# A fused cross-attention and MLP block on one core: the first unit's value matmuls moved between its scores, and half of the projection weights' low parts moved later on VectorE

## What is computed

```python
def reference_block(x, context, xa_mask, ...):        # x 2 x 2048 x 512, context 2 x 77 x 512, 16 heads of 32
    xq = layer_norm(x, qn_w, qn_b)
    ctx = layer_norm(context, cn_w, cn_b)
    q = (xq @ q_w)                                    # 512 x 512
    k, v = split(ctx @ kv_w)                          # 512 x 1024
    attn = softmax(where(xa_mask, -max, q . k * scale))   # over the 77 context rows, per head
    x = x + (attn . v) @ proj_w + proj_b
    h = layer_norm(x, n2_w, n2_b)
    return x + gelu(h @ fc1_w + fc1_b) @ fc2_w + fc2_b    # hidden size 2048
```

## Time and profile before

| | |
|---|---|
| device time, median of 3 runs | 1047.71 us (1047.18 to 1049.47) |
| profiled execution, its own time | 1051.2 us |
| its span | 1049.3 us |
| TensorE busy | 1033.1 us (98%) |
| VectorE busy | 822.3 us (78%) |
| ScalarE busy | 434.5 us (41%) |
| GpSimd busy | 359.2 us (34%) |

### The profile page before, as it was taken

One profiled execution on the slowest core, in us unless ns is written; L12 is line 12 of the kernel. 1 busy time (PEld: TensorE's weight loads), 2 busy tenths in 40 slices (PEclk: granted clock), 3 DMA queues, 4 the chain that ended last, 5 costly groups with the idle time before them and its releaser, 6 DMA issues.

```text
span 1049.3 us, 16369 instructions
## 1 busy us (share of the span) xinstructions
PE 1033.1 (98%) x5857; PEld 857.7 (82%) x5857; DVE 822.3 (78%) x1323; ACT 434.5 (41%) x766; POOL 359.2 (34%) x259
## 2 busy tenths in 40 slices
PE   8999999999999999999999999999999999999998
PEld 6788888888888777888778888878888888888887
DVE  7899999999997898887877676676766677666655
ACT  4344344444444566445533343342433352232221
POOL 3466566667787673233404000303100310300000
PEclk9999999999999999999999999999999999999999
DMA  7012122122210277564557535345536343834312
GB/s 267 8 47 71 51 92 74 63 62 83 81 42 22 74 297 233 188 232 160 197 213 258 225 131 191 124 159 174 227 131 234 118 164 126 312 120 172 124 67 81
DMA packets 52800, 149.33 MB, mean 142 GB/s; under 512 B 11313, under 2 KB 19545, under 8 KB 44531
## 3 DMA queue, kind: packets, MB, share of 16 engines
q1 hardware_dynamic: 52139, 147.25, 39.3%
q10 hardware_dynamic: 584, 1.06, 0.3%
HBM read 108.13 MB, written 39.85 MB: 141 GB/s over the span
## 4 chain that ended last, share of the span: by engine, by line
PE 93%; DVE 4%; issue 1%; DMA 0%; ACT 0%; POOL 0%; SPq 0%; DVEq 0%; ACTq 0%
PE bank L1801 32%; PE bank L1771 28%; PE bank L1604 8%; PE bank L1648 8%; PE bank L1585 5%; PE bank L1636 4%; PE bank L1617 3%; PE bank L1780 1%; PE bank L1595 1%; PE bank L1567 1%; PE bank L1625 1%; DVE acc L1409 1%; DVE hop L1371 1%; DVE gT L1401 1%; DVE w1r L1366 1%
## 5 line engine op out<-in xcount | busy, mean ns | idle before, releaser
L1801 PE MATMUL bank<-w2r,gT 128*128 128x512 f32 x1536 | 359.7, 391 | 2.2 <-DVE acc L1409 2.0
L1801 PEld LDWEIGHTS bank<-w2r,gT 128*128 128x128 f32 x1536 | 286.7, 188 | 64.2 <-DVE acc L1409 5.1
L1771 PE MATMUL bank<-hop,w1r 128*128 128x512 f32 x1344 | 314.2, 392 | 4.0 <-DVE hop L1371 3.0
L1771 PEld LDWEIGHTS bank<-hop,w1r 128*128 128x128 f32 x1344 | 252.3, 189 | 58.2 <-issue 4.9
L1409 DVE TENSOR_TENSOR acc<-bank,acc 128x512 f32<-128x512 f32 x256 | 176.7, 691 | 103.8 <-PE bank L1801 97.9
L1396 DVE TENSOR_TENSOR ybuf<-bank,ybuf 128x512 f32<-128x512 f32 x224 | 148.6, 688 | 82.3 <-PE bank L1771 74.2
L1046 ACT ACTIVATE ybuf<-ybuf,cols 128x512 f32<-128x512 f32 x128 | 91.6, 716 | 155.5 <-DVE ybuf L1396 155.5
L684 POOL TENSOR_TENSOR S<-S,rsum 128x1232 f32<-128x1232 f32 x32 | 75.3, 2354 | 61.6 <-DVE rsum L1202 61.6
L1401 DVE TENSOR_TENSOR gT<-ybuf,gT 128x512 fp32r<-128x512 f32 x128 | 92.9, 747 | 0.0
L649 POOL TENSOR_TENSOR hrs<-hve,mhalf 128x1 f32<-128x1 f32 x32 | 18.0, 562 | 213.6 <-DVE hve L1381 213.6
L792 POOL TENSOR_TENSOR acc<-acc,fc2b 128x512 f32<-128x512 f32 x32 | 44.0, 1391 | 134.7 <-DMA acc<-x_scratch 134.6
(11 more groups left out here) (111 smaller groups left out, 1450.8 us busy)
## 6 DMA issues: line engine op xcount, KB each, us to landing
w1r<-w_scratch SPq DMA_DIRECT2D x24, 1792.0 KB, 7.3
w2r<-w_scratch SPq DMA_DIRECT2D x24, 1024.0 KB, 5.4
w_scratch<-w1r SPq DMA_DIRECT2D x8, 1792.0 KB, 6.2
xr<-in_x SPq DMA_DIRECT2D x32, 256.0 KB, 2.9
x_scratch<-xr SPq DMA_DIRECT2D x32, 256.0 KB, 2.0
hring<-x_scratch SPq DMA_DIRECT2D x32, 256.0 KB, 3.0
acc<-x_scratch SPq DMA_DIRECT2D x32, 256.0 KB, 4.0
w_scratch<-w2r SPq DMA_DIRECT2D x8, 1024.0 KB, 4.9
```

The lines of the kernel that those rows point to most:

```text
L1771: mm = pe.matmul(bank_[:, :], w1r[:, w1_slot(s), c, w, kk * P:(kk + 1) * P], hop[i][:, d, kk, :], start=(kk == 0 and n == 0), stop=(kk == ...
L1801: mm = pe.matmul(bY[t % 2][:, :], gT[s % 2][:, j, d, t * P:(t + 1) * P], w2r[:, s % 2, j, w, :], start=(n == 0), stop=(n == 5))
```

## The change

Two edits, both in the preparation. On TensorE `values(0)` moves ahead of `x_T(1)`: it stood after the fourth score of tile 0, and now stands after the second. On VectorE two of the four `wpl` instructions stay where all four were (`prep="q"`, ahead of `q_lo(0)`), and the other two go into `prep="scores"`, between `q_lo(0)` and `exp_sum(1)`.

```diff
@@ vector_program, step, prep == "q"
                 keys_lo(1)
                 q_bias()
-                proj_weights(range(KT))
+                proj_weights((0, 1))
                 q_lo(0)
@@ vector_program, step, prep == "scores"
                 recip(0)
                 q_lo(0)
+                proj_weights((2, 3))
                 exp_sum(1)
@@ tensor_program, step, prep == "scores"
                 score(0, 0)
                 score(0, 1)
+                values(0)
                 x_T(1)
                 score(0, 2)
                 score(0, 3)
-                values(0)
                 for g_ in range(KT):
```

## The result

The changed kernel takes 1051.87 us (median of 7 runs, 1051.36 to 1052.66), the one before 1047.18 us (7 runs, 1046.09 to 1049.47). The ratio is 1.0047, with a 95% interval of 1.0036 to 1.0058: 4.7 us slower. In a second comparison the same changed kernel gave 1.0051 (1.0035 to 1.0066). The forecast was 1053.4 us.

A forecast was written before the change was run, and what follows sets the result against it. TensorE was taken to bound the loop, with VectorE nearly the bound in the preparation. Terms 0.0 (waits ahead of q) + 3.8 (wpl beside probs(0)) + 1.9 (clock) = +5.7 us on 1047.7 gave 1053.4 us, range 1049.4 to 1055.3.

The forecast's parts named there:

- TensorE has no slack in the loop: Loop: TensorE, busy for all 60.00 us from 60 to 120 us, can't hide a late start at its first score.
- Edit 1 and 2 sum to zero at q: Preparation, TensorE ahead of q: two waits of 1.5 us come back as one of 1.8 us, sum 0.0 us.
- The two wpl beside probs(0): VectorE ahead of exp_sum(1): wpl and GpSimd's probs(0) take turns, 3.46 us; exp_sum(1) and first score +3.8 us.
- edit 2: values(0) earlier on TensorE: masked(0, 2) and what follows it on VectorE and GpSimd come 1.67 us later.
- the bounds 0.7 and 6: Limits on the +3.8 us at exp_sum(1): 0.7 with normed() clear of GpSimd, 6 with a further GpSimd turn.
- The clock: Start of the loop: TensorE idle 3.9 us, then its granted clock falls, +1.9 us; bounds 0 and twice that.
- the row at 702 us: Earlier trace, loop: 2.29 us wait before 702.63, clock 0.50 behind it; 42 matmuls take 11.46, not 9.52 us, price 1.94.
- Sum: Whole kernel: 0.0 + 3.8 + 1.9 = +5.7 us on the median 1047.71, giving 1053.4 us.
- Rival B: Start of the loop: late start but the clock stays, 3.8 us alone, 1051.5 us; chance 0.18.
- A: Start of the loop: late start and the clock falls, the forecast itself, 1053.4 us; chance 0.55.
- C: VectorE beside probs(0): wpl hidden, only 1.67 us left, no clock drop, 1049.4 us; chance 0.13.
- D: Preparation, TensorE: both waits go, 1.5 us, and nothing comes in their place, 1046.2 us; chance 0.04.

The follow-up runs named there:

- e4: The changed kernel, but GpSimd begins probs(0) only when all four wpl are done; ratio to before 1.0009 (0.9997 to 1.0022).
- e8: The kernel before with all four wpl on GpSimd, behind its rstd of the preparation's second step; ratio to before 0.9993 (0.9979 to 1.0006).
- e3: The changed kernel with 14 identity matmuls (28 passes) in TensorE's gap ahead of the loop's first score; ratio to before 1.0039 (1.0026 to 1.0052).
- e5: The changed kernel with the second wpl pair between masked(0,1) and masked(0,2), in VectorE's idle time; ratio to before 1.0023 (1.0007 to 1.0038).
- e1: The kernel before with only the wpl edit, values(0) staying where it was; 1049.09 against 1047.46 us, ratio 1.0008 (0.9994 to 1.0023).
- e6: The kernel before with all four wpl on GpSimd, ahead of its rstd in the preparation; ratio to before 1.0049 (1.0035 to 1.0064).
- e2: The kernel before with only the values edit, all four wpl early as before; ratio to before 1.0020 (1.0007 to 1.0034).
- e7: As e6, with a quarter of values(0) ahead of x_T(1) and normed() ahead of masked(0,2); ratio to before 1.0060 (1.0044 to 1.0076).
- e9: As e8, with a quarter of values(0) ahead of x_T(1) and normed() ahead of masked(0,2); 1045.84 against 1048.10 us, ratio 0.9984.
- c1: The changed kernel run again, compared with the kernel before; ratio 1.0051 (1.0035 to 1.0066).

## Why the prediction was right, point by point

- **TensorE has no slack in the loop.** Right. From the first score to the end of the span it takes 998.2 us in e4, 998.5 in e8, 998.6 in e3 and e5, 998.7 in the values edit, wherever the start lies between 46.14 and 49.52 us. The traces that differ by more hold a piece of low clock: 1000.3 in the changed kernel (+1.65), 1002.1 before, 1002.2 in e1 and 1001.9 in e6, all three with a wait and a clock as in the earlier trace rows. In the second trace of the changed kernel it is 1001.2 us, 1.6 of them the clock. Against the first trace 1.0 us more is lost between 566 and 579 us, at a TensorE wait of 0.53 us for VectorE's hring that the first doesn't have; why it came is open.
- **Edit 1 and 2 sum to zero at q.** Two waits of 1.5 us were to come back as one of 1.8; it is 1.55. From `x_T(1)` to the end of the last score it took 35.51 + 0.30 - 32.68 = 3.13 us where I had 3.01, and q followed the end of `x_lo(1)` (37.31) in 0.05 us where I had counted 0.14; the rest is that VectorE was late by 1.59 us, not 1.67. q starts at 37.36 - 24.98 = 12.38 us after the copy, and at 37.93 - 25.41 = 12.52 before: 0.14 us gained, 0.0 forecast.
- **The two wpl beside probs(0).** Right in kind, some 0.2 us too dear. I had 2.25 + 2 x 0.605 = 3.46 us from the end of `less_max(1)`; it is 47.78 - 44.52 = 3.26. With the smaller shift of edit 2 (1.59) `exp_sum(1)` is 3.47 us late, not 3.8. That is 0.3 us too much, as far off as the clock; the bounds 0.7 and 6 held it. e4 shows the cause.
- **The clock.** Right in kind; +1.61 us where the row at 702 us gave 1.94. Why one fall was 0.3 us dearer than the other I can't tell. That the idle time is the cause rests on e3, and on e1, e2, e4 and e5, whose gaps of 1.56 to 1.80 us at the same place left the clock at 1.00. But the forecast had this term from a single row, and said that the trace has one wait near to 3.9 us. It has another: TensorE waits 2.61 us for a DMA at the start, longer than the 2.29 of the earlier trace rows, and its clock stays at 1.00 behind it (row in the last section). So that 3.9 us is longer than the wait that cost the clock was a weaker reason than it looked, and part of the hit is luck.
- **Sum.** +5.7 forecast, +5.1 in the traces, +4.7 in the medians. The forecast time is 1.5 us too high: 0.6 from the terms, 0.4 from the medians against the traces, and 0.5 as it was added to 1047.71, the median of three runs, where seven gave 1047.18. Rival B (the clock stays) would have been 1051.5, close to the measured 1051.87. So the time alone would have spoken for the wrong rival, and that it came within 1.5 us of the forecast is no proof of the mechanism; the windows at 51 to 54 us speak for A. Rivals C and D fall with the 3.34 us of the pair and with the 1.55 us ahead of q.

## What to carry to other kernels

A matmul group moved into a wait of TensorE can cost as much as it sticks out of it: 3.4 us of values in a wait of 1 us brought the loop's start 2.25 us later (e2), as VectorE, the engine that was really the bound, then had to wait. Cut the group to the length of the wait. When an instruction with two SBUF operands moves on VectorE, ask what GpSimd does at the new place, and when one moves to GpSimd, ask who waits for the next thing in GpSimd's list.

## What the runs showed of the hardware

- In the preparation the granted clock stayed at 1.00 behind TensorE waits of 1.54 to 1.80 us (e1, e2, e4, e5). It fell to 0.5 behind 3.43 us (two traces of the changed kernel), in or behind 5.71 and 5.69 us (e6, e7), and near 702 us behind 2.29, 2.26 and 2.17 us (before, e1, e6).
- The length of the wait doesn't decide alone. At 7 to 8 us TensorE waits for a DMA in every trace. Behind 2.61, 2.59, 2.39 and 2.02 us (before, changed, e5, e1) the clock stayed at 1.00; behind 2.48, 2.33, 2.31, 2.19 and 1.99 us (e3, e9, c1, e4, e8) it is 0.5 for some microseconds. What else decides, these runs don't show. This piece lies ahead of the copy of the q bias, so the table's measure leaves it out and the times of the runs don't. The wait and the window behind it before, and a window of e4:

```profile
7.96 0.33 PE L1523 MATMUL bank<-ident,rows 40*128 40x40 f32 x1 [2.61 <-DMA rows<-in_L_xattn_cn_w]
```

```profile
8.00:12.00 4.00, 4.00 (x21) 3.86 (x21) 2.88 (x9) 0.72 (x1) 0.61 (x1) 1.00 1.05 399
```

```profile
10.00:15.00 5.00, 5.00 (x19) 3.13 (x19) 4.64 (x13) 3.71 (x8) 2.42 (x4) 0.50 1.08 361
```

- One fall of the clock at the start of the loop cost 1.6 us (54.56 - 50.25 = 4.31 us for work that takes 2.70), and in the one trace with 28 passes on the identity in the gap, 3.29 us long, it didn't come.
- When VectorE had two instructions with two SBUF operands queued beside one of GpSimd, they took turns: in the changed kernel one wpl ran first, then GpSimd's, which had waited 0.5 us, then the second wpl. The wpl pair cost 3.26 us from start to start in place of 1.21, 2.05 us more, which is nearly all of the 2.25 that GpSimd's instruction takes alone.
